# A decoder of two layers: the recurrence's second product is made in layer 0's feed-forward part, and the last part's first norm and whole numbers in cross attention 1

## The chip, the cores and the metric

The kernel runs on one core of one Trainium2 chip. The metric is the device time of one execution in microseconds (us). The core has five engines with a queue each, which work in the order of their programs and wait for one another by semaphores: TensorE (PE; its weight loads are PEld), VectorE (DVE), ScalarE (ACT), GpSimd (POOL) and SyncE (SP, which here only starts DMAs).

## What is computed

Input x is 4 x 1024 x 256 in f32, and a context of 4 x 77 x 192. Each of the two layers adds an attention part, a cross attention and a feed-forward part to x, with a norm after each:

```python
x = _layernorm(x + _L0_attn_ref(x, ...))     # causal attention, keys and values rounded
x = _layernorm(x + _L0_xattn_ref(x, ctx))
x = _layernorm(x + _L0_ffn_ref(x, ...))      # rounded weights and inputs, depthwise convolution, silu
x = _layernorm(x + _L1_attn_ref(x, ...))     # the recurrence below
x = _layernorm(x + _L1_xattn_ref(x, ctx))
x = _layernorm(x + _L1_ffn_ref(x, ...))

def _L1_attn_ref(x, A, B_w, B_b, C_w, C_b, D_w, D_b):
    Bu = x @ B_w.T + B_b
    Du = x @ D_w.T + D_b
    state = tanh(state * exp(A) + Bu[:, t])      # for t in 0..1023
    return states @ C_w.T + C_b + Du

def _L1_ffn_ref(x, ...):
    h = layernorm(x, ln1_g, ln1_b)               # with gain and bias
    h = bitlinear(h, w1, b1)                     # h rounded to 127 levels by its row maximum, w1 to -1, 0, 1
    h = gelu(h)
    h = layernorm(h, ln2_g, ln2_b)
    return bitlinear(h, w2, b2)
```

## The kernel before

The 4096 tokens are 32 tiles of 128 (NT = 32), kept in the SBUF tensor `X` (128 x 32 x 256, f32). The stages follow one another with barriers: projections, self attention, cross attention 0, layer 0's feed-forward part (`ffn0_and_recurrence`), the keys and cross attention 1 (`cross_layer1`), and the last part (`ffn1`). Each of the last three is a loop over slots j, written once for every engine; in slot j an engine works on several tiles at different depths (`a = j`, `b = j - 1`, and so on), and the order of the lines in each engine's function is the order of its queue. Nothing is reordered.

In `ffn0_and_recurrence` tile d = j - 4 ends the chain: the second product (L1462), the norm into `X[:, d]`, two transposes of it (L94), a copy `xT` by VectorE (L1531), the product with `BwT` (L1479) into bank 3, and VectorE writes it with a bias into `R.BU` (L1547), which feeds the recurrence. Behind L1479 in TensorE's queue stand, in the next slot, eight bf16 transposes of `f_hq` and eight f32 transposes of `f_g`, whose row maximum VectorE takes first (L140, `qF_amax`).

The recurrence is 1024 steps of two ScalarE operations on 128x1 (L763), the second half of the batch interleaved with the first. `R.act_states(n)` issues the next n steps; calls are strewn over the stages, 18 steps a slot in layer 0's part, 90 beside the keys and 15 a slot in cross attention 1.

In `cross_layer1` tile c = j - 1 is the recurrence's output: its `X` tile is turned (L94), copied by ScalarE (`iT`, L1717), multiplied by `DwT` (L1643, into bank 7), the states by `CwT` are added (L1645), VectorE adds `ib` (the tile plus constants, made by GpSimd, L1748) at L1687 and norms it into `X` (L128). Tile f = j - 3 is turned for the scores, sc = j - 4 has its scores (L1636), their maximum (L1690), subtraction (L1694) and exponential (L1727), p = j - 5 the sum (L1681), the division on GpSimd (L1742), eleven transposes (L1673) and a copy (L1735), and o = j - 6 the product of 11 f32 pieces into bank 7 (L1661), the addition of `xb` (L1703) and the norm. Both c and o use bank 7, so L1661 waits for L1687. Beside this the weights of the last part are rounded: `Ternary.pool` puts one step of half a weight matrix on GpSimd in six slots for each of the two (L702, L705, L710), `Ternary.pe` and `Ternary.act` turn and copy them.

`ffn1` waits for six vectors (`vec_in`). Tile a = j has the first norm with gain and bias (VectorE L111, L116, L118 and L128, GpSimd L123, L1930, L1933), b = j - 1 the maximum, scale and rounding to whole numbers (`q1`, L140 to L155), the turn, the first product (L1820) and the dequantising L1882, followed by Gelu; c = j - 2 the second norm (L1871, L1878), d = j - 4 the second rounding (`q2`), transposes and product L1828, and e = j - 5 the sum `j_y` (L1847) and the last norm. Each norm's reciprocal root is a power on GpSimd (L123, 128x1).

## Time and profile before

| | us |
|---|---|
| median of 3 runs | 2395.96 (2391.68 to 2397.53) |
| profiled execution, time | 2395.88 |
| its span, first to last instruction | 2394.2 |
| mean granted TensorE clock | 0.838 of full |

| busy in the span | us | share |
|---|---|---|
| TensorE matmuls | 1779.7 | 74% |
| VectorE | 1818.2 | 76% |
| ScalarE | 1348.5 | 56% |
| GpSimd | 884.4 | 37% |

```profile
## 2 busy tenths in 40 slices
PE   8849999999867777865556556568999998345544
DVE  4678888888348888867999999345666654799998
ACT  2105666666723443431588888999998942233333
POOL 2510000000038668543343333005535532455553
PEclk9958999999959988976777777569999999567666
```

Each digit is the busy share in one fortieth of the span (59.9 us) in tenths, and PEclk the TensorE clock that was granted. Layer 0's feed-forward part is about the slices 19 to 26 (1080 to 1530 us), the keys and cross attention 1 are 27 to 34 (to 2030 us), the last part 35 to 40. No engine is full over the whole; in each stage another one is, and so the profile has to be read stage by stage and within a stage by slots.

### The profile page before, as it was taken

How to read it: one execution, taken by the hardware profiler on the slowest of the kernel's cores; microseconds unless marked ns; L12 is line 12 of the kernel's file. 1: busy time of each engine (PE TensorE's matmuls, PEld its weight loads, DVE VectorE, ACT ScalarE, POOL GpSimd, SP SyncE). 2: the span in 40 equal slices, each digit the busy share in tenths (PEclk: the TensorE clock that was granted, in tenths of full speed). 3: DMA queues.
4: the chain of work that ended last, by engine and by line, in shares of the span. 5: the costliest groups of instructions: out<-in, count | busy, mean ns of one | idle time of the engine just before them, and what ended most of it. 6: DMA issues, size and time to landing. Idle time of an engine off the chain costs nothing. (4 is left out here: it accounts for less than half of the span.)

```text
span 2394.2 us, 36511 instructions
## 1 busy us (share of the span) xinstructions
PE 1779.7 (74%) x12168; PEld 1122.0 (47%) x12168; DVE 1818.2 (76%) x4605; ACT 1348.5 (56%) x3379; POOL 884.4 (37%) x951
## 2 busy tenths in 40 slices
PE   8849999999867777865556556568999998345544
PEld 4513333333346666654444444245667676133333
DVE  4678888888348888867999999345666654799998
ACT  2105666666723443431588888999998942233333
POOL 2510000000038668543343333005535532455553
PEclk9958999999959988976777777569999999567666
DMA  2011111111010000000000000100000000000000
GB/s 77 18 25 29 30 29 29 29 29 29 13 59 12 30 12 12 10 1 18 11 8 1 1 1 1 34 18 1 18 1 1 1 1 8 28 14 14 12 14 18
DMA packets 42808, 41.55 MB, mean 17 GB/s; under 512 B 16054, under 2 KB 34670, under 8 KB 42622
## 3 DMA queue, kind: packets, MB, share of 16 engines
q1 hardware_dynamic: 42622, 39.23, 6.1%
q8 instruction: 97, 1.59, 0.3%
q14 instruction: 89, 0.73, 0.1%
HBM read 22.03 MB, written 4.19 MB: 11 GB/s over the span
## 5 line engine op out<-in xcount | busy, mean ns | idle before, releaser
L763 ACT ACTIVATE ST<-ST,aexp 128x1 f32<-128x1 f32 x2046 | 583.1, 376 | 3.7 <-PEq L57 3.7
L597 ACT ACTIVATE PT<-PS 128x512 f32<-128x512 f32 x576 | 309.8, 597 | 219.5 <-PE PS L482 188.6
L558 DVE CUSTOM_DVE_ANT_0 junk<-PS,maskw 128x128 bf16<-128x128 f32 (+3 forms) x512 | 226.4, 486 | 33.8 <-PE PS L459 33.8
L459 PE MATMUL PS<-KT,QT 48*128 48x512 bf16 (+3 forms) x768 | 190.4, 351 | 54.1 <-DMA QT<-QS 33.0
L94 PE MATMUL PS<-ident,j_t 128*128 128x128 f32 x320 | 76.6, 423 | 170.8 <-ACT j_t L1900 142.2
L94 PE MATMUL PS<-ident,X 128*128 128x128 f32 x320 | 77.0, 328 | 154.4 <-DVE X L128 139.0
L561 DVE TENSOR_REDUCE MX<-PS 128x1 f32<-128x512 f32 x256 | 164.5, 684 | 27.7 <-PE PS L459 24.9
L501 PE MATMUL PS<-PT,VP 128*32 128x256 f32 (+1 forms) x2560 | 184.2, 370 | 0.0
L1661 PE MATMUL PS<-L_xattn_VW,l_pT 112*128 112x256 f32 x704 | 159.4, 382 | 9.3 <-DVE i_xb L1687 6.5
L631 POOL TENSOR_SCALAR nm<-MX 128x16 f32<-128x16 f32 x32 | 6.5, 203 | 431.1 <-DVE MX L564 431.1
L123 POOL TENSOR_TENSOR n_rs<-n_ve,neghalf 128x1 f32<-128x1 f32 x96 | 104.7, 1107 | 151.7 <-DVE n_ve L118 151.7
L459 PEld LDWEIGHTS PS<-KT,QT 48*128 48x128 bf16 x768 | 58.4, 94 | 200.2 <-issue 80.4
L94 PEld LDWEIGHTS PS<-ident,j_t 128*128 128x128 f32 x320 | 62.9, 222 | 183.4 <-ACT j_t L1900 152.5
L1661 PEld LDWEIGHTS PS<-L_xattn_VW,l_pT 112*128 112x128 f32 x704 | 131.2, 190 | 32.0 <-issue 12.1
L1636 PE MATMUL PS<-Q,l_xT 128*128 128x512 f32 (+1 forms) x384 | 141.0, 517 | 2.4 <-DVE l_s L1694 2.4
L476 PE MATMUL PS<-QT,KT 51*128 51x512 bf16 (+3 forms) x768 | 136.7, 331 | 0.0
L94 PEld LDWEIGHTS PS<-ident,X 128*128 128x128 f32 x320 | 40.2, 159 | 187.8 <-DVE X L128 152.7
L1209 PE MATMUL PS<-ident,d_s 128*112 128x128 f32 x352 | 66.1, 335 | 82.5 <-POOL d_s L1398 57.2
L1573 POOL TENSOR_TENSOR f_c<-f_h,f_cw 128x1024 f32<-128x1024 f32 x32 | 61.0, 1907 | 158.7 <-DVE f_h L1542 158.7
L1366 ACT COPY d_pT<-PS 112x768 f32<-112x768 f32 x32 | 25.5, 798 | 136.8 <-PE PS L1209 136.7
L1636 PEld LDWEIGHTS PS<-Q,l_xT 128*128 128x128 f32 x384 | 70.8, 194 | 66.0 <-issue 66.0
L1398 POOL TENSOR_TENSOR d_s<-d_s,d_den 128x1232 f32<-128x1232 f32 x32 | 71.9, 2247 | 79.2 <-DVE d_den L1313 79.2
(311 smaller groups left out, 4476.2 us busy)
## 6 DMA issues: line engine op xcount, KB each, us to landing
KT<-KS SPq DMA_DIRECT2D x192, 32.0 KB, 2.0
QT<-QS SPq DMA_DIRECT2D x192, 32.0 KB, 2.0
xs<-in_x SPq DMA_DIRECT2D x8, 512.0 KB
cx<-in_x SPq DMA_DIRECT2D x32, 128.0 KB, 2.0
out<-j_xn SPq DMA_DIRECT2D x32, 128.0 KB, 1.7
QT<-NMT SPq DMA_DIRECT2D x192, 2.0 KB
f_raw<-in_L_ffn_w SPq DMA_DIRECT2D x2, 1024.0 KB, 5.4
j_raw<-in_L_ffn_w SPq DMA_DIRECT2D x2, 1024.0 KB, 5.2
```

The costliest lines, as they stand in the source:

```text
L94: last = T.transpose(dst[:, i * P:(i + 1) * P], src[:, i * P:(i + 1) * P], idm[:, :])
L123: G.tensor_tensor(self.rs[u][:, :], self.ve[u][:, :], neghalf[:, :], ALU.pow).then_inc(self.rstd_done, 1)
L459: T.matmul(bank(u % 3)[:, 0:w * P], QT[i % R][rows, qt * P:(qt + 1) * P], KT[i % R][rows, k0 * P:(k0 + w) * P], start=True, stop=True).the ...
L476: last = T.matmul(bank(3 + (u0 + e) % 3)[:, at:at + w * P], KT[i % R][rows, kt * P:(kt + 1) * P], QT[i % R][rows, q0 * P:(q0 + w) * P], st ...
L501: last = T.matmul(bank(6 + first // 4)[32 * h:32 * h + 32, first % 4 * P:(first % 4 + hi - lo) * P], VP[:, v0:v0 + 32], PT[n % 4][:, h, lo ...
L558: V.tensor_tensor_reduce(junk[u % 3][:, 0:w * P], bank(u % 3)[:, 0:w * P], maskw[:, BANK - w * P:], 1.0, NEG, ALU.add, ALU.max, MX[i % 2][ ...
L561: V.tensor_reduce(MX[i % 2][:, e, slot:slot + 1], bank(u % 3)[:, 0:w * P], AX.X, ALU.max).then_inc(m_done, 1)
L597: C.activation(PT[n % 4][:, 2 * pr + e, 0:w], bank(3 + u % 3)[:, 0:w], ACT.Exp, scale=0.25).then_inc(e_done, 1)
L763: C.activation(self.ST[:, m, t:t + 1], self.ST[:, m, t - 1:t] if t else self.zero[:, :], ACT.Tanh, bias=self.BU[:, m, t:t + 1], scale=self ...
L1398: G.tensor_tensor(by_head(s[p % 4][:, :]), by_head(s[p % 4][:, :]), over_keys(den[p % 4]), ALU.mult).then_inc(d_p, 1)
L1636: last = T.matmul(PS[:, c0:end], xT[sc % 2][:, k * P:(k + 1) * P], x.M[:, k, sc % B, c0:end], start=k == 0, stop=k == KD - 1)
L1661: last = T.matmul(bank(7)[:, 0:D], pT[o % 2][:, i * P:(i + 1) * P], x.VW[:, i, o % B, :], start=i == 0, stop=i == VN - 1)
```

## The change

The product of X with D is made in layer 0's part. There TensorE multiplies the same `xT` by `DwT` behind the product with `BwT`, and VectorE adds the result to `X[:, d]`, with a new semaphore `f_du` that the next tile's second product also waits for, since both use bank 3. In cross attention 1 the transposes, the ScalarE copy and the D product of tile c fall away; what is left of it, the product of the states with `CwT`, goes to the front of TensorE's slot and into the free half of bank 3. The rings `ib`, `iT` and `xb` fall away too: the additions are made in `X` in place.

In the room that this frees cross attention 1 makes, for tile r = j - 7, the last part's first norm in one VectorE operation (gain times a reciprocal root that GpSimd works out from the variance already known, three operations on 128x1) and the bias on GpSimd, and for q = j - 8 the row maximum, scale and rounding, kept as bf16 in `JQ` with the levels in `LV`. The stage has one slot more. The last part starts from `JQ`: its first norm and first rounding are gone, its tiles are one to two slots closer together (NT + 3 slots instead of NT + 6), and the order of its VectorE operations within the slot changes. It waits for four vectors; the other two are loaded in cross attention 1.

The diff, cut to its core:

```diff
@@ ffn0_and_recurrence: pe, dve
                     if d >= 1:
                         T.wait_ge(R.fed, d)
+                        T.wait_ge(f_du, d)
...
                     for k in range(KD):
-                        last = T.matmul(bank(3)[rows(d), D:D + P], R.BwT[:, k, :], xT[d % 2][:, k * P:(k + 1) * P],
-                                        start=k == 0, stop=k == KD - 1)
+                        T.matmul(bank(3)[rows(d), D:D + P], R.BwT[:, k, :], xT[d % 2][:, k * P:(k + 1) * P],
+                                 start=k == 0, stop=k == KD - 1)
+                    for k in range(KD):
+                        last = T.matmul(bank(3)[:, 0:D], xT[d % 2][:, k * P:(k + 1) * P], R.DwT[:, k, :], start=k == 0, stop=k == KD - 1)
                     last.then_inc(f_bmm, 1)
...
+                    V.tensor_add(X[:, d, :], bank(3)[:, 0:D], X[:, d, :]).then_inc(f_du, 1)
@@ cross_layer1: sp, pe
+            for d, n in ((g1, "ln1_g"), (b1, "ln1_b")):
+                SP.dma_start(d[:, :], row("L1_ffn_" + n)).then_inc(vec_in, 16)
...
+                w1.pe_free(j - 1)
+                w2.pe_free(j - 1)
                 if on(c):
-                    transposes(X[:, c, :], bank(7), KD).then_inc(i_tr, 1)
+                    rows = slice(64 * (c % 2), 64 * (c % 2) + 64)
+                    T.wait_ge(R.step, 2 * P * (c // B + 1))
+                    if c >= 1:
+                        T.wait_ge(i_y, c)
+                    T.matmul(bank(3)[:, D:2 * D], R.ST[rows, (c % B) // 2, (c // B) * P:(c // B) * P + P], R.CwT[rows, :],
+                             start=True, stop=True).then_inc(i_mm, 1)
...
-                if on(c):
-                    T.wait_ge(i_xT, c + 1)
-                    for k in range(KD):
-                        T.matmul(bank(7)[:, 0:D], iT[c % 2][:, k * P:(k + 1) * P], R.DwT[:, k, :], start=k == 0, stop=False)
...
+                if c >= 0:
+                    T.wait_ge(i_y, min(c + 1, NT))
...
-                    if on(c):
-                        T.wait_ge(i_y, c + 1)
-                    else:
+                    if o >= 1:
                         T.wait_ge(d_y, o)
@@ cross_layer1: dve (new order: c's addition first, then p, sc, c's norm, o, q and r between)
                 if on(c):
                     V.wait_ge(i_y, c + 1)
-                    nI.dve_stats(c, ib[c % 2])
+                    nI.dve_stats(c, X[:, c, :])
                     nI.dve_moments(c)
-                    nI.dve_apply(c, X[:, c, :], ib[c % 2][:, :]).then_inc(i_xn, 1)
+                if on(q):
+                    V.wait_ge(l_b, q + 1)
+                    qJ.dve_max(q, l1[q % 2][:, :])
+                if on(c):
+                    nI.dve_apply(c, X[:, c, :], X[:, c, :]).then_inc(i_xn, 1)
+                if on(q):
+                    qJ.dve_level(q)
                 if on(o):
                     V.wait_ge(d_mm, o + 1)
                     V.wait_ge(d_xb, o + 1)
-                    V.tensor_add(xb[o % 4][:, :], bank(7)[:, 0:D], xb[o % 4][:, :]).then_inc(d_y, 1)
+                    V.tensor_add(X[:, o, :], bank(7)[:, 0:D], X[:, o, :]).then_inc(d_y, 1)
+                if on(q):
+                    qJ.dve_inverse(q)
...
+                if on(q):
+                    qJ.dve_scale(q, tmp[:, :], l1[q % 2][:, :])
+                if on(r):
+                    V.wait_ge(d_xn, r + 1)
+                    V.wait_ge(l_rs, r + 1)
+                    V.scalar_tensor_tensor(l1[r % 2][:, :], X[:, r, :], rs[r % 2][:, :], g1[:, :], ALU.mult, ALU.mult).then_inc(l_g, 1)
+                if on(q):
+                    qJ.dve_round(q, JQ[:, q, :], tmp[:, :]).then_inc(l_q, 1)
+                if on(o):
+                    nD.dve_apply(o, X[:, o, :], X[:, o, :]).then_inc(d_xn, 1)
@@ cross_layer1: act, pool
-                R.act_states(3)
-                if on(c):
-                    C.wait_ge(i_tr, c + 1)
-                    C.copy(iT[c % 2][:, :], bank(7)[:, 0:D]).then_inc(i_xT, 1)
-                R.act_states(6)
+                R.act_states(9)
...
                 if on(o):
                     nD.pool_rstd(o)
+                    if o >= 2:
+                        G.wait_ge(l_g, o - 1)
+                    G.wait_ge(nD.rstd_done, o + 1)
+                    G.tensor_scalar(ve[o % 2][:, :], nD.mv[o % 4][:, 1:2], nD.rs[o % 4][:, :], nD.rs[o % 4][:, :], ALU.mult, ALU.mult).then_inc(l_var, 1)
+                    G.wait_ge(l_var, 2 * o + 1)
+                    G.tensor_scalar(ve[o % 2][:, :], ve[o % 2][:, :], 1.0, EPS, ALU.mult, ALU.add).then_inc(l_var, 1)
+                    G.wait_ge(l_var, 2 * o + 2)
+                    G.tensor_tensor(rs[o % 2][:, :], ve[o % 2][:, :], neghalf[:, :], ALU.pow).then_inc(l_rs, 1)
+                if on(f):
+                    G.wait_ge(d_tr, f + 1)
+                    G.tensor_tensor(X[:, f, :], X[:, f, :], bo[:, :], ALU.add).then_inc(d_xb, 1)
+                if on(r):
+                    G.wait_ge(l_g, r + 1)
+                    G.tensor_tensor(l1[r % 2][:, :], l1[r % 2][:, :], b1[:, :], ALU.add).then_inc(l_b, 1)
                 w1.pool(j)
                 w2.pool(j)
@@ ffn1: the tiles of a slot; the order of VectorE's operations
-                b, d = j - 1, j - 4
+                b, d = j, j - 2
...
-                    transposes(t1[b % 2], bank(0), KD).then_inc(j_tr, 1)
+                    transposes(JQ[:, b, :], bank(0).bitcast(BF16), KD).then_inc(j_tr, 1)
...
-            for j in range(NT + 6):
-                a, b, c, d, e = j, j - 1, j - 2, j - 4, j - 5
+            for j in range(NT + 3):
+                b, c, d, e = j, j - 1, j - 2, j - 3
...   # d's maximum and levels, e's j_y as before
+                if on(c):
+                    V.wait_ge(j_gelu, c + 1)
+                    n2.dve_stats(c, h[c % 3])
                 if on(e):
                     V.wait_ge(n_y, e + 1)
                     n3.dve_stats(e, y[e % 2])
...   # moments of c, moments of e, then c's L1871
+                if on(e):
+                    n3.dve_apply(e, xn[e % 4][:, :], y[e % 2][:, :]).then_inc(n_xn, 1)
                 if on(c):
                     V.wait_ge(n2.rstd_done, c + 1)
...   # c's L1878, b's L1882
-                    q1.dve_scale(b, t1[b % 2][:, :], l1[b % 4][:, :])
...
-                    n1.dve_apply(a, l1[a % 4][:, :], X[:, a, :]).then_inc(j_ln, 1)
```

## Rows read from the trace of the kernel before

**Rows 1.** Table of windows, one in each of three stages; us, busy us (instructions) by engine, granted clock, DMA.
```profile
1200.00:1300.00 100.00, 61.32 (x414) 49.23 (x412) 93.50 (x246) 87.36 (x291) 38.79 (x33) 0.75 0.00 1
1800.00:1927.00 127.00, 124.59 (x558) 89.74 (x557) 83.51 (x143) 114.02 (x339) 67.81 (x56) 1.00 0.00 1
2200.00:2360.00 160.00, 81.11 (x339) 51.69 (x337) 153.63 (x380) 57.40 (x61) 86.15 (x94) 0.69 0.04 13
```

**Rows 2.** Timeline, one slot of layer 0's part: start, us, engine, line, idle before.
```profile
1371.97 1.11 PE L1479 MATMUL PS<-f_xT,BwT 128*64 128x128 f32 x4 [0.83 <-DVE f_xT L1531]
...
1373.84 1.91 PE L94 MATMUL PS<-ident,f_g 128*128 128x128 f32 x8
...
1375.80 1.22 DVE L140 TENSOR_REDUCE qF_amax<-PS 128x1 f32<-128x1024 f32 x1 [0.64 <-PE PS L94]
...
1385.18 1.11 PE L1479 MATMUL PS<-f_xT,BwT 128*64 128x128 f32 x4 [0.83 <-DVE f_xT L1531]
```

**Rows 3.** Table of windows, two microseconds of that slot, for the granted clock.
```profile
1374.00:1375.00 1.00, 1.00 (x7) 1.00 (x6) 0.94 (x3) 1.00 (x5) 1.00 (x1) 0.50 0.00 0
1376.00:1377.00 1.00, 1.00 (x16) 0.94 (x14) 1.00 (x2) 1.00 (x5) 1.00 (x1) 1.00 0.00 0
```

**Rows 4.** Line L1643: ns least/median/most of one record.
```profile
L1643 PE MATMUL PS<-DwT,i_xT x128: 379/379/797, 1592.2 to 1974.7; 128*128 128x256 f32 x128
```

**Rows 5.** Timeline, its first block of four records in cross attention 1.
```profile
1592.16 2.08 PE L1643 MATMUL PS<-DwT,i_xT 128*128 128x256 f32 x4 [9.98 <-ACT i_xT L1717]
```

**Rows 6.** Timeline, TensorE in one slot of cross attention 1.
```profile
1778.78 0.38 PE L94 MATMUL PS<-ident,X 128*128 128x128 f32 x2
...
1783.14 1.03 PE L1643 MATMUL PS<-DwT,i_xT 128*128 128x256 f32 x4
...
1784.72 0.44 PE L94 MATMUL PS<-ident,X 128*128 128x128 f32 x2
...
1785.40 0.89 PE L1661 MATMUL PS<-L_xattn_VW,l_pT 112*128 112x256 f32 x3 [0.24 <-DVE i_xb L1687]
```

**Rows 7.** Table of windows, one whole slot of cross attention 1.
```profile
1841.17:1853.82 12.65, 12.41 (x57) 8.95 (x56) 8.70 (x15) 11.44 (x36) 8.45 (x7) 1.00 0.00 1
```

**Rows 8.** Timeline, ScalarE's copy of tile c in that slot.
```profile
1845.29 0.35 ACT L1717 COPY i_xT<-PS 128x256 f32<-128x256 f32 x1
```

**Rows 9.** Timeline, GpSimd in that slot.
```profile
1843.09 3.70 POOL L702 TENSOR_SCALAR j_raw<-j_raw,j_w2T_inv 128x1024 f32<-128x1024 f32 x1
...
1852.82 0.73 POOL L1748 TENSOR_TENSOR i_xb<-X,cd 128x256 f32<-128x256 f32 x1
```

**Rows 10.** Timeline, starts of two slots and the drained end of the last part.
```profile
2208.27 1.28 DVE L1871 SCALAR_TENSOR_TENSOR Q<-Q,n_mv,j_g 128x1024 f32<-128x1024 f32 x1
...
2218.63 1.28 DVE L1871 SCALAR_TENSOR_TENSOR Q<-Q,n_mv,j_g 128x1024 f32<-128x1024 f32 x1
...
2368.05 1.28 DVE L1882 SCALAR_TENSOR_TENSOR Q<-PS,j_ds,j_bh 128x1024 f32<-128x1024 f32 x1
...
2369.56 1.21 DVE L140 TENSOR_REDUCE q_amax<-Q 128x1 f32<-128x1024 f32 x1
...
2374.08 1.28 DVE L1871 SCALAR_TENSOR_TENSOR Q<-Q,n_mv,j_g 128x1024 f32<-128x1024 f32 x1
2374.24 2.05 POOL L123 TENSOR_TENSOR n_rs<-n_ve,neghalf 128x1 f32<-128x1 f32 x2 [6.91 <-DVE n_ve L118]
...
2375.81 1.28 DVE L1878 SCALAR_TENSOR_TENSOR Q<-Q,n_rs,j_b 128x1024 f32<-128x1024 f32 x1 [0.44 <-POOL n_rs L123]
...
2377.33 1.21 DVE L140 TENSOR_REDUCE q_amax<-Q 128x1 f32<-128x1024 f32 x1
```

**Rows 11.** By lines, the norm of c: busy us, mean ns; idle before it, releaser.
```profile
L128 DVE TENSOR_SCALAR X<-i_xb,nI_mv,nI_rs 128x256 f32<-128x256 f32 x32 | 25.8, 806 | 21.4 <-POOL nI_rs L123 21.4
```

**Rows 12.** Timeline, VectorE's first operation of the last part, with its wait.
```profile
2040.01 0.43 DVE L111 BATCH_NORM_STATS2 n_six<-X 128x6 f32<-128x256 f32 x1 [8.41 <-DMA j_bo<-in_L_ffn_b]
```

**Rows 13.** Line L1847: ns least/median/most, start of the first and of the last.
```profile
L1847 DVE SCALAR_TENSOR_TENSOR j_y<-PS,j_ds,j_xb x32: 472/474/485, 2079.5 to 2388.9; 128x256 f32<-128x256 f32 x32
```

More of the change, by code:

```diff
@@ L1801, in pe @@
         def pe():
-            for j in range(NT + 5):
-                b, d = j - 1, j - 4
+            for j in range(NT + 2):
+                b, d = j, j - 2
                 if on(d):
@@ L1904, in act @@
                         C.wait_ge(j_mm, b - 1)
-                    C.activation(xqT[b % 2][:, :], bank(0)[:, 0:D], ACT.Identity, bias=down[:, :], scale=1.0).then_inc(j_xqT, 1)
+                    C.copy(xqT[b % 2][:, :], bank(0).bitcast(BF16)[:, 0:D]).then_inc(j_xqT, 1)
                 if on(d):
@@ L1923, in pool @@
                 if on(a):
-                    n1.pool_rstd(a)
                     if a >= 6:
```

150 lines of the change are left out of this document (56 added, 94 removed).

## Prediction

> **What bounds the kernel now.** I read the table of windows first [rows 1], because the three stages that the change touches have three different limits. In the feed-forward part of layer 0 VectorE is busy 93.5 us of 100 and TensorE 61.3 at a granted clock of 0.75. In cross attention 1 TensorE is busy 124.6 us of 127 at full clock, ScalarE (the recurrence's tanh) 114.0, VectorE only 83.5 and GpSimd 67.8. In the last part VectorE is busy 153.6 us of 160. So moving VectorE work out of the last part into cross attention 1, and TensorE work out of cross attention 1 into layer 0's part, is sound if the cover is real; each of the three has to be priced from its own slot (one turn of the loop over j).
>
> **Layer 0's feed-forward part: the product X times D is added (loss).** The timeline of one slot [rows 2] shows VectorE waiting 0.64 us for the eight f32 transposes of f_g; they end at 1375.75 and the maximum starts at 1375.80. These transposes stand in TensorE's queue behind L1479, which can't start before the normed X is turned and copied. So from L1479 (1371.97) to the end of the transposes (3.8 us) TensorE is on the path, although it idles elsewhere in the slot, and the new matmuls are put exactly between. The window over it has the granted clock at 0.50, which is the lower level, 1.2 GHz; the one two us later has 1.00 [rows 3]. The same product in cross attention 1 has matmul records of 379 ns at best and 797 ns at worst [rows 4], and the block of four took 2.08 us at the lower level behind an idle TensorE [rows 5] and 1.03 us at the higher one [rows 6]. Behind L1479 there is no start-up, so I take 1.75 us at the lower level. Since TensorE works longer in one stretch, the clock will in some slots be up before the transposes of f_g are through; those took 1.91 us at the lower level [rows 2], so at most half of that comes back. Estimate: 0.4 us back on average, so +1.35 us a slot, with bounds of 1.0 (higher clock) and 1.75 (none back). The added VectorE addition on 256 columns is some 0.4 us, as the statistics of 256 columns [rows 12]; it lies in the wait that the longer TensorE stretch makes, and costs nothing; it also lets the next second product wait on f_du, which is long set by then. If the product cost nothing, that addition would cost its 0.4 us. 32 slots: **+43 us**, bounds +30 and +56.
>
> **Cross attention 1: what leaves.** TensorE's slot is 12.65 us with 12.41 busy [rows 7]. It loses the transposes of tile c (0.38 us, of which some 0.25 are not overlapped), the D product (1.03, some 0.95) and the wait for VectorE's i_xb in front of the big product: L94 starts at 1784.72 with 0.44 us of work, L1661 at 1785.40 [rows 6], 0.4 us more than it need. 12.65 - 0.25 - 0.95 - 0.4 = 11.05 us. The recurrence's engine is then next: ScalarE has 11.44 us in that slot and loses only the 0.35 us copy [rows 7, 8]. That gives 11.1 to 11.2; eight slots have a weight copy on top, so I take 11.4 us, a gain of 1.25 us.
>
> **Cross attention 1: what comes.** VectorE gets seven operations on 128x256 or smaller (maximum, scale, round, multiplication by the gain, and two on one column), five of some 0.4 us and two of some 0.15, 2.3 us. 8.70 busy [rows 7] becomes 11.0 without overlaps, and some 10.3 with them, since back-to-back operations overlap by about 0.1 us each. It is covered, barely. GpSimd gets two operations on one column, a third power of minus one half (two of the last part took 2.05 us together, the second alone about 0.5 [rows 10]) and an addition of 0.73 us [rows 9]: 1.7 us. In an ordinary slot it has 4.8 us of work (8.45 less the 3.70 of L702 [rows 7, 9]) and becomes 6.5. But in twelve slots it also carries a step of the weights' rounding, up to 3.70 us [rows 9]: 10.2 us, and in these it stops twice for VectorE (variance of c, variance of o) with VectorE waiting for it right behind. I price these two stops at 1 us each and take 12.4 us for those slots, a gain of 0.2. Of the 26 slots in which all stages run 11 are such. 15 x 1.25 + 11 x 0.2 = 21. At the start of the loop ScalarE's states set the pace and c's copy leaves, some 3.5 us; at its end one more slot is added, in which the last tile's gain, bias, maximum, scale and rounding run one after the other, also some 3.5 us. Together **-21 us**, bounds -40 (11.1 everywhere) and 0 (VectorE and GpSimd give all of it back). The two loads on SP's queue stand behind the first weights and ahead of a load that waits anyway; their first use is seven slots later. The wait on the recurrence's step moves to the front of TensorE's slot; the states are a chunk ahead there.
>
> **The last part: what leaves.** A slot takes 10.36 us (2208.27 to 2218.63 [rows 10]). The trace shows the new slot almost as it will be, because in the drained slots the first norm and its rounding are absent: from maximum to maximum 7.77 us (2369.56 to 2377.33), without the product's L1882, which adds 1.28 less its overlap, 1.20 [rows 10]. 8.97 us. Two corrections. In the new order the statistics of c don't wait behind those of e, 0.35 us less. And the order puts the norm of e right behind L1871: its power stands in GpSimd's queue behind c's, so it comes to run during L1871. In these rows a power that started 0.16 us into L1871 was through 0.4 us after it had ended (the pair took 2.05 us and L1878 waited 0.44). This stall is already in the 7.77; but once it ends GpSimd goes on at once with the addition of bo, and beside such an addition VectorE's norm of 256 columns takes 0.81 us [rows 11], twice the 0.4 that I have for 256 columns: +0.4. **9.05 us a slot**, bounds 8.5 (no contention) and 9.6.
>
> **The last part: the sum.** VectorE is released at 2040.0 after a wait of 8.41 us for the six vectors [rows 12]. The last L1882 starts at 2368.05 [rows 10], 328.0 us later. New: the whole numbers are there, so h(0) comes at 0.3 us, h(1) some 6.6 later, h(2) 8.8 later, then 29 slots of 9.05: 15.7 + 262.5 = 278.2, so 49.8 less. From L1882 to the last j_y there are 20.9 us now (to 2388.9 [rows 13]); the loop has one drained slot less, 3.7 off. Two vectors of 128 KB less of 1.9 MB in 8 us is 1.0 off. **-54.5 us**, bounds -38 (9.6) and -70 (8.5).
>
> **Against a rule of the skill.** L1878 starts at 2375.81, released by c's power; the pair of powers ends at 2376.29, so e's power started just before L1878, ran beside it in some 0.5 us, and L1878 took its usual 1.28 [rows 10]. Neither held the other up. The Trainium skill, "SBUF — State Buffer", section "SBUF: two separate sides", says that GpSimd and certain VectorE operations share one pair of ports as an exclusive lock, held for the whole instruction by whichever started first. By that rule the start of L1878 beside e's power should not have been possible, so the row speaks against it here; what it would make of the new order is the third rival.
>
> **The rivals.**
> 1. The product in layer 0's part is cheap, because the clock comes up early or doesn't fall between slots: 30 us instead of 43, 2350. For it: longer TensorE stretches. Against: the mean granted clock of this part is 0.75 although TensorE has a long stretch in every slot [rows 1], and the stretch priced here comes first after its idle time, at 0.50 [rows 3].
> 2. No contention in the last part, 8.5 us a slot: 29 x 0.55 = 16 less, 2347. Against it: the rows with 2.05 and 0.81.
> 3. The powers hold L1871 up too: c's power starts 0.16 us behind L1871 now [rows 10]; in the new order two operations of e, some 0.3 us, stand between the variance and L1871, so it will start some 0.15 us ahead of it. If L1871 has to wait for its rest, 0.5 less 0.15, and e's power with it, a slot is 9.5 us and the time 29 x 0.45 = 13 more, 2376. Against it: L1878 at 2375.81, as above.
> 4. Cross attention 1 gains nothing, 2384, because ScalarE, now next in line, waits for VectorE's subtraction, which is late by the seven operations.
> 5. Slower. In cross attention 1 GpSimd and VectorE hand over to each other four times a slot (two powers, the new variance, the bias), with VectorE's scale, gain and rounding in a row just when o's power wants to run. From 13.1 us a slot on the gain of the last part is eaten up (26 x 0.45 + 43 = 54.7 against 54.5); at 13.9 us, which is 1.5 us more than I have for the slots in which GpSimd rounds weights, 26 x 1.25 = 33 are lost and the time is 2417. Against it: the sum of VectorE's work is 10.3.
> 6. The change doesn't do what it says: the first product stays late in the slot. TensorE's program order excludes that.
>
> **The numbers.** 2395.9 + 43 - 21 - 54.5 = 2363.4. The profiled execution has a span of 2394.2 and a time of 2395.88, the median of the runs is 2395.96, so the sum needs no shift. Chances: forecast (2352 to 2374) 0.42, rival 1 0.14, rival 2 0.12, rival 3 0.10, rival 4 0.13, rival 5 0.07, a mixture about zero 0.02. A measurement of this kernel can tell about 0.3% from no change, 7.2 us. Of rival 4 and of losses that add up, 0.08 fall within that. Faster 0.85, same 0.08, slower 0.07. The range takes in rivals 1 to 4 and the bounds of the product: 2334 to 2392.
>
> **What would show it.** The interval between two starts of L1479's successor 14.6 us instead of 13.2 and a longer wait of qF_amax for TensorE; in cross attention 1 11.4 us between two results of the big product, with ScalarE busy nearly throughout, and 12.4 where GpSimd rounds weights; in the last part 9.05 us a slot, the idle time of VectorE in front of the norm of e with GpSimd's power as its releaser, and a first j_y some 19 us after the vectors have landed instead of 39.5. Wrong would be above all a slot of cross attention 1 over 12.6, or one of layer 0's part under 14.

## The result and the profile after

The changed kernel takes 2318.6 us (median of four runs, 2315.4 to 2322.4) beside 2396.7 for the kernel before (2391.7 to 2398.2): ratio 0.9678, 95% interval 0.9654 to 0.9702, 78 us less. The forecast was 33 us less, and its range ended at 2334. The profiled execution has a span of 2313.6 us, 80.6 under that of before. By the stages' first loads on SyncE's queue, which mark their starts:

| stretch | before | after | difference | forecast |
|---|---|---|---|---|
| to the start of cross attention 1 | 1581.7 | 1593.0 | +11.3 | +43 |
| cross attention 1 | 449.7 | 415.3 | -34.4 | -21 |
| last part | 362.8 | 305.3 | -57.5 | -54.5 |

Windows of the changed kernel, columns as in [rows 1]:

```profile
1200.00:1300.00 100.00, 63.87 (x403) 48.58 (x404) 88.80 (x247) 83.91 (x276) 36.25 (x33) 0.74 0.02 6
1800.00:1900.00 100.00, 97.56 (x429) 69.11 (x428) 79.16 (x181) 95.64 (x284) 77.13 (x86) 1.00 0.00 1
2100.00:2200.00 100.00, 57.27 (x250) 35.33 (x248) 92.73 (x180) 40.83 (x46) 28.84 (x35) 0.70 0.05 15
```

The limits are the same three engines. In layer 0's part VectorE's share fell by five points: it waits more, but not as much more as forecast. In the last part GpSimd fell from 54 to 29 in 100.

Timeline of the changed kernel, the slot that answers [rows 2]:

```profile
1380.73 1.12 PE L1480 MATMUL PS<-f_xT,BwT 128*64 128x128 f32 x4 [0.83 <-DVE f_xT L1534]
1381.77 2.07 PE L1483 MATMUL PS<-DwT,f_xT 128*128 128x256 f32 x4
...
1384.41 1.04 PE L94 MATMUL PS<-ident,f_g 128*128 128x128 f32 x8
...
1383.88 0.36 DVE L1550 TENSOR_SCALAR ST<-PS,bb 64x128 f32<-64x128 f32 x1 [1.34 <-PE PS L1483]
1384.27 0.42 DVE L1552 TENSOR_TENSOR X<-PS,X 128x256 f32<-128x256 f32 x1
...
1385.49 1.22 DVE L140 TENSOR_REDUCE qF_amax<-PS 128x1 f32<-128x1024 f32 x1
```

The product (L1483) takes 2.07 us, dearer than the 1.75 of the sum. But the transposes of f_g behind it take 1.04 us where they took 1.91, and the maximum follows with no wait. The granted clock over product and transposes, as in [rows 3]:

```profile
1382.00:1383.00 1.00, 1.00 (x3) 0.82 (x4) 0.55 (x2) 1.00 (x5) 0.37 (x1) 0.50 0.00 0
1384.60:1385.40 0.80, 0.80 (x8) 0.62 (x6) 0.80 (x3) 0.80 (x4) 0.79 (x1) 1.00 0.00 0
```

The product runs at the lower level (0.50), the transposes at the higher (1.00). VectorE's wait has moved: it no longer stands in front of the maximum but in front of L1550 (1.34 us), which waits until the product too is done.

One ordinary slot of cross attention 1 (answers [rows 7]) and, below it, one of the four long ones, from one start of the big product (L1663) to the next, in which GpSimd rounds weights:

```profile
1770.50:1781.63 11.13, 11.13 (x51) 8.05 (x50) 9.00 (x21) 11.13 (x35) 6.69 (x9) 1.00 0.01 2
1843.71:1855.75 12.04, 11.31 (x51) 7.96 (x50) 8.98 (x21) 11.06 (x34) 10.20 (x11) 1.00 0.00 1
```

TensorE has no idle time in the ordinary slot, nor has ScalarE; in the long one TensorE idles 0.73 us. The last part (answers [rows 10]):

```profile
2153.96 1.28 DVE L1884 SCALAR_TENSOR_TENSOR Q<-Q,n_mv,j_g 128x1024 f32<-128x1024 f32 x1
2155.75 0.73 DVE L128 TENSOR_SCALAR j_xn<-j_y,n_mv,n_rs 128x256 f32<-128x256 f32 x1 [0.51 <-POOL n_rs L123]
2156.41 1.27 DVE L1892 SCALAR_TENSOR_TENSOR Q<-Q,n_rs,j_b 128x1024 f32<-128x1024 f32 x1
```

and GpSimd beside it:

```profile
2153.85 1.80 POOL L123 TENSOR_TENSOR n_rs<-n_ve,neghalf 128x1 f32<-128x1 f32 x2 [6.45 <-DVE n_ve L118]
2155.62 0.72 POOL L1932 TENSOR_TENSOR j_xb<-X,j_bo 128x256 f32<-128x256 f32 x1
```

The pair of powers, the idle 0.51 us in front of e's norm and the long norm (0.73) are as forecast. First and last result, to set beside [rows 13]:

```profile
L1870 DVE SCALAR_TENSOR_TENSOR j_y<-PS,j_ds,j_xb x32: 473/475/484, 2035.3 to 2308.5; 128x256 f32<-128x256 f32 x32
```

The slot is 8.94 us.

### The profile page after: what moved, and what is told of

It is laid out like the page before. It is cut to its first block and busy times, and to the rows that moved or that the text cites. A ratio compares the mean times of both kernels' runs of the same rounds, so it can differ in the third digit from the quotient of the medians.

```text
span 2313.6 us, 36269 instructions
## 1 busy us (share of the span) xinstructions
PE 1758.1 (76%) x12104; PEld 1097.3 (47%) x12104; DVE 1782.5 (77%) x4542; ACT 1333.4 (58%) x3347; POOL 847.5 (37%) x983
## 5 line engine op out<-in xcount | busy, mean ns | idle before, releaser
L94 PE MATMUL PS<-ident,X 128*128 128x128 f32 x256 | 64.0, 339 | 143.7 <-DVE X L128 129.6
L1663 PE MATMUL PS<-L_xattn_VW,l_pT 112*128 112x256 f32 x704 | 157.4, 379 | 2.9 <-issue 2.9
L1663 PEld LDWEIGHTS PS<-L_xattn_VW,l_pT 112*128 112x128 f32 x704 | 131.2, 190 | 20.0 <-issue 3.4
L94 PE MATMUL PS<-ident,j_t 128*128 128x128 f32 x256 | 56.7, 394 | 109.8 <-ACT j_t L1906 109.8
L123 POOL TENSOR_TENSOR n_rs<-n_ve,neghalf 128x1 f32<-128x1 f32 x64 | 58.0, 922 | 214.8 <-DVE n_ve L118 214.8
L94 PEld LDWEIGHTS PS<-ident,X 128*128 128x128 f32 x256 | 35.1, 166 | 166.5 <-DVE X L128 143.1
L1563 ACT ACTIVATE f_g<-f_g 128x1024 f32<-128x1024 f32 x32 | 33.9, 1058 | 121.0 <-DVE f_g L1494 121.0
L94 PEld LDWEIGHTS PS<-ident,j_t 128*128 128x128 f32 x256 | 44.6, 203 | 121.0 <-ACT j_t L1906 121.0
```

What stands on the lines that cost most here:

```text
L94: last = T.transpose(dst[:, i * P:(i + 1) * P], src[:, i * P:(i + 1) * P], idm[:, :])
L123: G.tensor_tensor(self.rs[u][:, :], self.ve[u][:, :], neghalf[:, :], ALU.pow).then_inc(self.rstd_done, 1)
L1663: last = T.matmul(bank(7)[:, 0:D], pT[o % 2][:, i * P:(i + 1) * P], x.VW[:, i, o % B, :], start=i == 0, stop=i == VN - 1)
```

## Experiments: what the product costs in layer 0's part

**The change's first half alone.** The kernel before with the product moved and nothing of the norm:

```diff
 ffn0:   + D product behind the BwT product, tensor_add into X, f_du
 cross1: - transposes(X[:, c, :]), ScalarE's copy iT, the D product
         the product of the states with CwT stays behind the scores, in bank 7
```

> The kernel before with the first half of the change alone: D's product and the addition in layer 0's part, no transposes, no copy and no D in cross attention 1; the last part's first norm and whole numbers stay in the last part. If the two halves add up: +11.3 us up to the start of cross attention 1 as in the changed kernel, there 5 us from the start of the stage, 35.7 us from the slots and 4 us more because the norm's work is not in them, no longer tail, and nothing in the last part: 33 us shorter than before, 2362 to 2366. By the recorded sum (+43 in layer 0's part, 24.5 off in cross attention 1) the same kernel would take 2412 to 2418. If the slots of cross attention 1 gain only because the stage's VectorE order was written anew with the norm's work: 2380 to 2395.

Measured: 2373.2 us beside 2399.0, ratio 0.9894 (0.9868 to 0.9921), span 2370.5. The three stretches differ from before by +9.0, -34.0 and +1.3 us. So 23.7 us of the gain is the product's, and the norm's half brings the other 56.9 of the span (2370.5 to 2313.6) at no net cost to cross attention 1. The recorded sum had +43 - 24.5 for this half and would have been 42 us too high; for the norm's half it had 51 with its tail, 6 too few. **So most of the miss of 48 us lies in the product's half.** How much depends on a term that belongs to both: if the 12.4 us for the slots with rounding is charged to the norm's work, which was its reason, the halves missed by 31 and 17 us. My additive expectation of 2362 to 2366 was 9 us too low: this kernel's slots of cross attention 1 are 11.56 us and not 11.1, where TensorE keeps the old order, with a wait in it:

```profile
1763.87 0.70 PE L1644 MATMUL PS<-CwT,ST 64*128 64x256 f32 x2
1764.50 0.44 PE L94 MATMUL PS<-ident,X 128*128 128x128 f32 x2
1765.18 4.99 PE L1660 MATMUL PS<-L_xattn_VW,l_pT 112*128 112x256 f32 x22 [0.24 <-DVE i_xb L1686]
```

In the changed kernel the product of the states stands in front of the scores, and this wait is gone. A run further down that has the new order and none of the norm's work has ordinary slots of 11.13, so the 0.43 us come with the order (and the bank); which of its pieces brings them isn't shown beyond the wait of 0.24.

**No product, half of one, one, two; no addition.** The edits to the changed kernel:

```diff
 p0:  - the four matmuls with DwT (the addition stays)
 half:  matmul(bank(3)[:, 0:P], xT, DwT[:, k, 0:P])
 p1:  - tensor_add(X, bank 3, X), - T.wait_ge(f_du, d)
 p2:    for k in (0, 1, 0, 1): matmul(bank(3)[:, 0:D], ...)
```

> The changed kernel without the product of X with D in layer 0's part; the addition stays and adds whatever stands in the bank, so the last state is left out of the output's meaning. The changed kernel's slot is 13.66 us against 13.24 of the kernel before. Theory A (the 0.42 us are VectorE's addition, and the product is hidden): the slot stays at 13.6 to 13.7 and the time within 4 us of the changed kernel's 2318.6. Theory B (the 0.42 us are what is left of the product, the addition lies in VectorE's wait for the transposes of f_g): the slot falls to 13.2 to 13.3, the part ends 13 to 17 us earlier, and the time is 5 to 12 us shorter, since the recurrence's states on ScalarE set the end.

> The changed kernel with the product of X with D over half of D's columns alone (the other half of the addition adds what stood in the bank; the output is not the reference's). So far the slot of layer 0's part is 13.3 us with no product, 13.66 with one and 15.15 with two. If the cost grows in proportion up to one product (0.37 us for 1.98 us of TensorE): 13.45 to 13.5, and a time of 2309 to 2311. If the slot keeps with the pattern of the granted clock (13.66 with one product at two equal stretches of either level): half a product falls either to the 13.3 of none or to 13.6. If each microsecond before the transposes of f_g counted in full beyond a slack of 1.6 us: 13.3, the time of no product, 2301 to 2304.

> The changed kernel with the product of X with D but without VectorE's addition of its result and without TensorE's wait for it (the term D x is left out of the output). Theory A (the addition sets the slot): the slot falls from 13.66 to 13.2 to 13.3 us. Theory B (the product sets it): the slot stays at 13.6 to 13.7. If both matter: between.

> The changed kernel with the product of X with D issued twice over in each slot of layer 0's part (its result is then twice as large; 2.07 us more work at the lower clock, 1.03 at the higher). Theory A (a product in this place is hidden because the granted clock comes up before the transposes of f_g): the first product used the slack up, so the second costs 0.8 to 1.1 us a slot, at the higher clock: slot 14.5 to 14.8, time +25 to +35 us. Theory B (a product costs 0.42 us a slot, in proportion): slot 14.0 to 14.1, time +10 to +15 us. The recorded prediction's price, 1.35 to 1.75 us for each, would give 15.0 to 15.4 and +45 to +55 us.

(The second product doesn't double the result, as that expectation says: its sum starts anew and overwrites the first.) Measured (the four edited kernels in two runs each, with 2396.9 and 2399.1 us for the kernel before beside them). The second column is the mean interval over all 32 f_y. The slot and the columns behind it are means over the 21 slots from the eighth f_y to the twenty-ninth, in which the recurrence runs and nothing is drained:

| kernel | time | f_y, mean interval | slot | VectorE waits for TensorE | sixteen taps | D product | f_g transposes |
|---|---|---|---|---|---|---|---|
| before | 2396.7 | 12.99 | 13.31 | 0.74 | 5.33 | - | 1.84 |
| addition alone | 2301.4 | 12.99 | 13.30 | 0.53 | 5.29 | - | 1.88 |
| half | 2313.8 | 13.37 | 13.66 | 1.44 | 4.62 | 1.22 | 1.85 |
| one (changed) | 2318.6 | 13.50 | 13.66 | 1.44 | 4.63 | 2.07 | 1.06 |
| one, no addition | 2316.8 | 13.46 | 13.66 | 1.72 | 4.63 | 2.08 | 1.05 |
| two | 2360.7 | 14.82 | 15.15 | 3.02 | 4.63 | 3.56 | 1.19 |

Theory A fell: the addition costs nothing, as forecast. The price is the product's, and it is no line: 0.4 us a slot for half of it, nothing for the other half, 1.5 for a second one, which is more than the forecast had for the first. The second half is free because of the clock: 0.85 us more of product, 0.79 less of transposes. A second product finds them at the higher clock already and wins nothing. That left the first half: it adds 0.91 us of waits and the slot grows by only 0.36. The column that moves the other way is VectorE's sixteen steps of the convolution's outer taps, 0.67 us shorter.

**The taps and GpSimd.** Kernel before, VectorE's taps and maximum, and GpSimd's two steps of the middle tap:

```profile
1387.09 1.91 POOL L1573 TENSOR_TENSOR f_c<-f_h,f_cw 128x1024 f32<-128x1024 f32 x1 [5.00 <-DVE f_h L1542]
1389.07 1.90 POOL L1575 TENSOR_TENSOR f_c<-f_c,f_cb 128x1024 f32<-128x1024 f32 x1
...
1389.01 1.22 DVE L140 TENSOR_REDUCE qF_amax<-PS 128x1 f32<-128x1024 f32 x1 [1.01 <-PE PS L94]
1390.15 2.81 DVE L1491 SCALAR_TENSOR_TENSOR f_g<-f_h,f_cw,f_c 128x128 f32<-128x128 f32 x8
```

Changed kernel:

```profile
1382.63 1.90 POOL L1577 TENSOR_TENSOR f_c<-f_h,f_cw 128x1024 f32<-128x1024 f32 x1 [4.74 <-DVE f_h L1545]
1384.61 1.90 POOL L1579 TENSOR_TENSOR f_c<-f_c,f_cb 128x1024 f32<-128x1024 f32 x1
...
1386.63 2.18 DVE L1494 SCALAR_TENSOR_TENSOR f_g<-f_h,f_cw,f_c 128x128 f32<-128x128 f32 x8
```

GpSimd's steps start when f_h is made. Before, they run until 1390.97, and the first tap starts at 1390.15; of the eight, it alone is long, 969 ns against 340, so it lasts until just after GpSimd has ended. In the changed kernel the wait for the product stands between f_h and the taps, GpSimd is through at 1386.51, the taps start at 1386.63, and eight take 2.18 us instead of 2.81. By lines (ns least/median/most), the first taps of before, and then of the changed kernel:

```profile
L1491 DVE SCALAR_TENSOR_TENSOR f_g<-f_h,f_cw,f_c x184: 333/339/1417, 1203.4 to 1498.1; 128x128 f32<-128x128 f32 x184
```

```profile
L1494 DVE SCALAR_TENSOR_TENSOR f_g<-f_h,f_cw,f_c x176: 341/344/348, 1208.8 to 1497.6; 128x128 f32<-128x128 f32 x176
```

Before, the long tap is there in 22 of the 23 slots of this stretch, and in each of the 22 it ends 0.15 us behind GpSimd's step. In the changed kernel not one of 176 is long any more; GpSimd is through only 0.05 to 0.34 us before the first tap, a margin that nobody had planned. To test it, GpSimd's two steps were cut to 8 of 128 positions, with the product and without:

```diff
- G.tensor_tensor(c0[:, :, :],   h[:, :, 1:P + 1], cw, mult)   # and the same for the bias
+ G.tensor_tensor(c0[:, :, 0:8], h[:, :, 1:9],     cw, mult)
```

> Layer 0's part without the product of X with D, and with GpSimd's two steps of the convolution over 8 of 128 positions (product and most of the middle tap are left out; not the reference's output). Its twin without the second cut has a slot of 13.26 us, in which VectorE's sixteen steps of the outer taps take 5.38 us and the first eight run beside GpSimd's second step. Theory P (GpSimd in flight makes VectorE's taps slower, and the product's price is low because it moves the taps behind GpSimd's steps): the taps fall to 4.6 and the slot to 12.5 to 12.9. Rival (the taps' length follows something else, so the low price is the clock's alone): taps 5.3 to 5.4, slot 13.2 to 13.3.

> The changed kernel, product in its place, with the same cut of GpSimd's convolution steps (most of the middle tap is left out). The changed kernel has taps of 4.61 us already and a slot of 13.66. Theory P: with nothing left to win on the taps the slot stays at 13.5 to 13.7, so that without GpSimd in the way one product costs 0.8 to 1.1 us a slot, against 0.40 with it. Rival (the clock alone): the difference between this slot and its twin's without the product stays 0.4.

Measured: 2279.6 us without the product (slot 12.59, f_y every 12.35 us), 2310.3 with it (slot 13.66, 13.53), the slots again over the 21 full ones. With GpSimd out of the way **one product costs 1.07 us a slot**, as theory P said (0.8 to 1.1); with GpSimd's steps in place it costs 0.36. The difference is 0.71 us, and the taps account for it: without the product the sixteen take 4.63 us now instead of 5.29, and that slot falls from 13.30 to 12.59. The rival, the clock alone, is out: these two keep the clock's pattern (transposes of f_g 1.86 and 1.06 us) and not the low price. Over the whole kernel one product costs 30.6 us here and 17.2 with GpSimd's steps. That is more than 21 slots explain, since the first seven intervals of f_y, in which the recurrence is only starting, grow by 1.6 and 0.75 us each; no run shows why. The long first tap is gone:

```profile
L1494 DVE SCALAR_TENSOR_TENSOR f_g<-f_h,f_cw,f_c x176: 341/345/348, 1207.9 to 1474.3; 128x128 f32<-128x128 f32 x176
```

**The product taken off the path.** Same work, the product a slot later, behind the transposes of f_g; its addition behind the maximum:

```diff
 TensorE: hq transposes(d), f_g transposes(c),
+         wait R.fed > e; D product(e = d - 1)
          second product(d), first product(a), ..., BwT product(d)
 VectorE: maximum(c)
+         wait f_dmm > e; tensor_add(X[:, e, :], bank 3)
          taps
```

> The changed kernel with the same work, but the product of X with D issued one slot later, behind the transposes of f_g, and its addition behind the maximum over them. Theory P and the path (a product costs only what it puts before the transposes of f_g, and VectorE's wait for them): the slot falls to 13.2 to 13.4 as with no product, the time to 2298 to 2306. Rival (the addition now waits for the product, up to 2 us at the lower clock, and the second product of the feed-forward part comes late for f_y): slot 13.7 to 14.6, time 2318 to 2345.

Measured: 2311.4 us, f_y every 13.28 us; the slots run between 13.0 and 13.8, 13.49 over the 21 full ones. Somewhat under half of what the product costs is won back (7.2 of 17.2 us), less than expected. VectorE waits 0.33 us for the late product and 0.71 for the transposes, and the held tap is back in 7 of 22 slots, each time ending 0.14 to 0.15 us behind GpSimd's step:

```profile
L1496 DVE SCALAR_TENSOR_TENSOR f_g<-f_h,f_cw,f_c x176: 335/344/1744, 1206.9 to 1492.1; 128x128 f32<-128x128 f32 x176
```

## Experiments: cross attention 1 and the last part

**Without the norm's work in cross attention 1.**

```diff
- VectorE: gain, maximum, scale, round; GpSimd: variance, power, bias; one slot
+ VectorE once: memset(JQ), memset(LV)
```

> The changed kernel without the last part's first norm and whole numbers in the slots of cross attention 1 (they are left out; the last part works on ones). Theory 1 (TensorE alone sets the slot of 11.35 us, the added work of VectorE and GpSimd is free): the slots stay at 11.3 to 11.4, only the tail behind the last slot is 4 to 6 us shorter: time 5 us shorter. Theory 2 (the added work delays the slots, by GpSimd's powers and VectorE's rounding): slots of 10.9 to 11.1 and the slots with the weights' rounding at 11.4 instead of 12.1: time 15 to 20 us shorter.

Measured: 2307.6 us. By the starts of TensorE's big product (L1663), the four slots of 12.04 to 12.20 fall to 11.13 and the ordinary ones stay at 11.13; those with a weight's transposes have 11.36 to 11.44, and one 11.84. From the first big product to the last there are 338.1 us instead of 342.1, and from there to the end of the stage 9.2 instead of 15.3. (The fill of JQ takes VectorE 6.9 us at the start; the 25 us wait described below absorbs it.) So the added work costs some 4 us in the slots and 6 in the tail, 10.3 of the stage and 11.0 of the time. That lies between the theories: in the ordinary slots the work is free (theory 1), in the long ones it isn't (theory 2).

**GpSimd's rounding steps at 64 of 1024 columns.**

```diff
- G.tensor_scalar(half(raw, k), half(raw, k), inv, 1.0, mult, min)     # and the two like it
+ G.tensor_scalar(half(raw, k)[:, 0:64], half(raw, k)[:, 0:64], inv, 1.0, mult, min)
```

> The changed kernel with GpSimd's twelve steps of rounding the last part's weights over 64 of 1024 columns (most of the weights is left out, the output is not the reference's). In cross attention 1 eight slots take 12.05 to 12.2 us where the others take 11.3. Theory G (GpSimd's long steps hold up what GpSimd owes the slot: the power of the norm, the division): these eight slots fall to 11.3 to 11.4, the stage ends 5 to 7 us sooner. Theory T (TensorE's and ScalarE's own work for the weights, or the DMA, makes them long): they stay at 12.0 to 12.2.

Measured: 2312.9 us. The long slots fall to 11.13 (theory G; where the weights' transposes begin, one slot takes 12.02). The expectation counts eight; by TensorE's big product there are four, the other steps of rounding leave the slot at 11.1 to 11.4. In the long slots of the changed kernel the division stands behind a step of 3.6 to 3.7 us, and TensorE's transposes of its result wait for it, 0.73 to 0.89 us:

```profile
1843.40 3.64 POOL L705 TENSOR_SCALAR j_raw<-j_raw 128x1024 f32<-128x1024 f32 x1
1847.01 2.25 POOL L1760 TENSOR_TENSOR l_s<-l_s,l_den 128x1232 f32<-128x1232 f32 x1
1849.35 1.38 PE L1675 MATMUL PS<-ident,l_s 128*112 128x128 f32 x11 [0.73 <-issue]
```

With the norm's work left out the same steps of rounding cause no such wait, so it takes both. The stage gains 3.9 us (411.4 for 415.3). The time of the profiled execution hardly shows it, because the stage starts 3.3 us later there; 2.2 of these are already there at the first f_y, ahead of anything that the edit touches.

**ScalarE's states dealt out otherwise.** At the start of cross attention 1 in the changed kernel ScalarE works off 54 steps before it copies the first turned tile:

```profile
1593.06 30.14 ACT L763 ACTIVATE ST<-ST,aexp 128x1 f32<-128x1 f32 x108 [1.02 <-PEq L57]
1623.12 0.34 ACT L1741 COPY l_xT<-PS 128x256 f32<-128x256 f32 x1
```

```diff
 ffn0:   act_states(9) twice a slot  ->  act_states(10) twice
 cross1: 9 + 3 + 3 a slot            ->  0 in slots 0 to 3, then 9 + 3 + 3
```

> The changed kernel with the same work, but the recurrence's states dealt out otherwise on ScalarE: 20 instead of 18 in a slot of layer 0's part, none in slots 0 to 3 of cross attention 1 (where 54 of them, 30 us, stand ahead of the first copy of transposed tokens, which TensorE waits 25 us for). Theory S (the states set that start and ScalarE has room in layer 0's slot of 13.66): cross attention 1 has its fifth recurrence product 18 to 22 us sooner, layer 0's slot stays at 13.7, and the time is 2296 to 2302. Rival: ScalarE becomes the bound of layer 0's slot (20 states 11.4 us, silu 1.06, the weights' copy 0.6 to 0.8: about 13.1, with its waits over 13.66): slot 13.9 or more, 7 to 10 us of the gain lost, time 2303 to 2312.

Measured: 2299.0 us. The interval between VectorE's third and fourth addition of a recurrence product falls from 24.99 to 3.70 us; layer 0's slot stays at 13.66. ScalarE had the room.

**The order in the last part.** Two edits, together and one by one:

```diff
 late apply: VectorE ..., L1884, L1892, L1896 (h), then the norm of e
 w1 first:   TensorE transposes JQ(b), product w1(b), then transposes t2(d), product w2(d)
             ScalarE copy xqT(b) before t2(d)
```

> The changed kernel with two changes of order in the last part: VectorE applies the last norm behind h instead of before the second step of the second norm, and TensorE and ScalarE make the transposes and the w1 product of tile b before the transposes of t2. Theory V (VectorE's chain sets the slot of 8.94: it waits 0.51 for the power of the last norm and 0.3 for the w1 product): slot 8.0 to 8.3, time 2292 to 2298. Rival (the ring from h through Gelu on ScalarE, the second norm, t2, its transposes and y sets it, and the new order lengthens that by making t2 wait behind the copy): slot 8.6 to 9.0, time 2310 to 2319. Slower, if TensorE's w1 product at the lower clock (1.9 us) comes in front of the transposes of t2 each time: slot over 9.0.

> The changed kernel with only VectorE's last norm applied behind h in the last part. Its wait for the power (0.51 us) goes; the slot of 8.94 falls to 8.4 to 8.5 if nothing stands behind it; to 8.6 to 8.8 if TensorE's w1 product, which then ended 0.3 us before h, comes late next.

> The changed kernel with only TensorE's and ScalarE's order changed in the last part (w1's product of tile b before the transposes of t2). If VectorE's wait for the power is the only one in the slot, it stays at 8.9 to 9.0; the gain of 0.73 us a slot with both would then be mostly the other edit's. If the order alone carries it: 8.2 to 8.5.

Measured: both 2296.0 us, slot 8.21. Order alone (one run): 2315.4, slot 8.94, nothing. Late apply alone (one run): 2317.0, slots between 8.20 and 9.03, 8.7 on average; in a slot of 9.02 VectorE waits 0.72 us for the w1 product in front of h. Its last part is 7.7 us shorter all the same (297.6 for 305.3); the time doesn't show it, because the stages ahead, which the edit leaves as they are, took longer in that run (first f_y 5.6 us later). **They remove two waits that end nearly together: alone they pay nothing and 0.24 us a slot, both 0.73.** VectorE in the version with both:

```profile
2102.34 1.28 DVE L1884 SCALAR_TENSOR_TENSOR Q<-Q,n_mv,j_g 128x1024 f32<-128x1024 f32 x1
2103.72 1.28 DVE L1888 SCALAR_TENSOR_TENSOR Q<-Q,n_rs,j_b 128x1024 f32<-128x1024 f32 x1
2104.93 1.28 DVE L1892 SCALAR_TENSOR_TENSOR Q<-PS,j_ds,j_bh 128x1024 f32<-128x1024 f32 x1
2106.12 0.40 DVE L128 TENSOR_SCALAR j_xn<-j_y,n_mv,n_rs 128x256 f32<-128x256 f32 x1
```

No wait is left, and the norm of e takes 0.40 us, GpSimd being quiet beside it.

**Together**, without and with the late product:

> The changed kernel with both reorderings together: the states dealt out otherwise (19.5 us shorter alone) and the two changes of order in the last part (22.6 us alone). If they are independent: 2275 to 2279, a ratio to the kernel before of 0.949 to 0.951. If one takes the other's gain (the last part's slot rises again, or the stages between give it back): 2285 to 2296.

> The kernel with the states dealt out otherwise and the two changes of order in the last part (2280.1 us), and the product issued one slot later as in the run before this one. If the late product wins 12 to 17 us alone and ScalarE's 20 states a slot (11.4 us, with silu and a copy about 13.1) find room in a slot of 13.3: 2263 to 2269. If ScalarE then sets the slot: 13.5 or more and 2270 to 2280.

Measured: 2280.1 us, ratio to before 0.9503 (0.9482 to 0.9524), and **2272.5 us, 0.9482 (0.9466 to 0.9498)**, the fastest here, 46 us under the changed kernel. The first lacks 3.7 us of the sum of the single gains (19.6 and 22.6, of two runs each). In its start of cross attention 1 TensorE idled 4.12 us and then ran at the lower clock:

```profile
1627.20 2.60 PE L1675 MATMUL PS<-ident,l_s 128*112 128x128 f32 x11 [4.12 <-ACT l_xT L1741]
1629.72 1.22 PE L1639 MATMUL PS<-CwT,ST 64*128 64x256 f32 x2
1630.87 5.83 PE L1648 MATMUL PS<-Q,l_xT 128*128 128x512 f32 x12
```

where the version with the states alone idled 2.45 us and stayed at the higher one:

```profile
1626.25 1.41 PE L1675 MATMUL PS<-ident,l_s 128*112 128x128 f32 x11 [2.45 <-ACT l_xT L1741]
1627.59 0.70 PE L1639 MATMUL PS<-CwT,ST 64*128 64x256 f32 x2
1628.22 4.40 PE L1648 MATMUL PS<-Q,l_xT 128*128 128x512 f32 x12
```

The difference, 3.1 us, is most of the 3.7. The version with the late product has the same 4.12 us of idle time there and the same slow stretch (2.60, 1.22 and 5.70 us). It wins 7.6 us by the late product instead of 12 to 17; its slot is 13.49, with VectorE's waits as in the late product's own run.

## Why the prediction was wrong, step by step

The forecast was 48 us too high: 32 of them in layer 0's part, 13 in cross attention 1, 3 in the last part.

**Layer 0's part, +43 forecast, +11.3 measured: the step that failed.** Its slot is 13.66 us and not 14.6, one of the two signs of being wrong that the forecast named.
- *Price of the product, 1.75 us at the lower clock.* It took 2.07 in every slot; right in kind, too low.
- *"At most half comes back, 0.4 us on average."* Mis-sized. The transposes went from 1.84 to 1.06 us, 0.78 back. With the longer stretch the rise comes ahead of them in nearly every slot; I took the scatter of before for the scatter of after. The two errors nearly cancel: with some 0.2 us of overlap the maximum starts 1.06 us later behind the start of the product with `BwT` (4.81 us for 3.75, means of 21 slots), where the forecast had 1.35.
- *The path ends at the maximum.* Here the forecast missed a term, and this is most of the miss. It followed TensorE to the maximum and not VectorE beyond it, where the first tap was held until GpSimd's step had ended (969 ns for 340). The product's wait lets GpSimd finish: 0.70 us a slot. 1.06 - 0.70 is 0.36, and the slot grew by 0.35. Without GpSimd's steps the product costs 1.07 a slot, as much as the maximum is late there (4.82 for 3.74).
- *VectorE's addition costs nothing.* Right, by the run without it (13.66 either way) and the one without the product (13.30, for 13.31 before).
- *32 slots.* The part's last f_y is 15.0 us later, cross attention 1 starts 11.3 later. That the stage between absorbs the rest was not in the sum; by the mean interval, 0.51 us times 31 are 15.9.

**Cross attention 1, -21 forecast, -34.4 measured.**
- *Start, 3.5 us:* 5.0. *Tail, +3.5:* +6.2.
- *Slots.* From TensorE's first big product to its last 377.7 us became 342.1, 35.6 less or 1.37 us a slot over the 26 in which all stages run; the forecast had 21. The 1.25 that I took for ordinary slots was too little: 12.65 became 11.13, and with a weight's transposes 13.07 or 12.87 became 11.36. Mis-sized above all was the rest: I gave 0.2 us to 11 slots in which GpSimd rounds weights. Four were long, 12.04 to 12.20 instead of 12.4, and gained 0.5 us each; the other steps of rounding cost next to nothing. The wait was also another than the one priced: not VectorE's for a power, but TensorE's for the division, which GpSimd makes late.
- *ScalarE as the next bound.* Both are without a gap in the ordinary slot, but TensorE sets it: past the last state ScalarE is busy only 2.9 to 3.5 us of a slot, and the slots keep their 11.13 and 11.34.

**The last part, -54.5 forecast, -57.5 measured.** Right term by term, within some tenths. Slot 8.94 for 9.05; the vectors' wait 6.96 instead of 8.41 (1.45 less for 1.0); last h to last j_y 16.8 us for 17.2; h(0) at 0.9 us instead of 0.3. The stall in front of e's norm is 0.51 us and the norm 0.73 beside GpSimd's addition.

**The rivals.** Rival 1 (cheap product, 2350) is what happened, and further: its reason, the clock, is the smaller part of it, and I gave it 14 in 100 and only 13 us. Rival 2 fell: the contention in the last part is there, and taking it out brings 8.21 together with TensorE's order. Rival 3 fell: the pair of powers started 0.11 us ahead of L1884 (2153.85, 2153.96), and L1884 took its usual 1.28. Rival 4 fell: cross attention 1 gained 34 us. Rival 5 fell: past the start no slot of cross attention 1 is over 12.2 us by TensorE's big product. Rival 6 fell.

**VectorE and GpSimd in each other's way.** Measured: a first tap that starts 0.82 us before GpSimd's step ends takes 969 ns, 340 otherwise, and between 1203 and 1498 us such taps take up to 1417. A held tap ends 0.15 us behind GpSimd's end. That is what the Trainium skill, "SBUF — State Buffer", section "SBUF: two separate sides", says of VectorE operations with two SBUF inputs beside a GpSimd operation that reads SBUF: whichever starts first has the port pair for the whole instruction. By that rule the trace of this stage agrees. The forecast had set it aside on the strength of powers on one column and didn't ask it of the two 1.9 us steps in layer 0's part. For those powers the rows go one way against it and one way with it. A power that is already running doesn't hold VectorE (L1884 at 1.28 with a power begun 0.11 us ahead). But a power that starts while VectorE's 1.28 us step is running does wait: it takes 0.55 us otherwise, and here 1.54 in the kernel before (beside L1871, which starts at 2103.96) and 1.28 in the changed one (beside L1884, from 2153.96), each time ending 0.4 us after VectorE's step:

```profile
2104.12 1.54 POOL L123 TENSOR_TENSOR n_rs<-n_ve,neghalf 128x1 f32<-128x1 f32 x1 [3.83 <-DVE n_ve L118]
```

```profile
2154.36 1.28 POOL L123 TENSOR_TENSOR n_rs<-n_ve,neghalf 128x1 f32<-128x1 f32 x1
```

The second of these is the power that e's norm waits 0.51 us for. So the stall that the forecast took from its rows as a length (2.05 for the pair) is this hold; with 0.55 us the power would have been through before L1884 was. The maximum, which reads bank memory, took its usual 1.22 beside GpSimd.

## What to carry to other kernels

When work is put in front of a wait, follow the waiting engine on to its next operations: what it now starts later may come clear of a neighbour that held it up, and that part of the wait is free. Price the first dose and not a line: here half a product, one and two cost 0.4, 0.4 and 1.9 us a slot. Count slots only where the loop is full: a stretch that takes in the drained end makes the slot look shorter. If two waits in a slot end nearly together, try the edits that remove them together before judging either.

## What the runs showed of the hardware

- VectorE's step on two SBUF tensors, begun while GpSimd has a 1.9 us step in flight, lasts until 0.15 us after that step's end (340 ns becomes 969, at most 1417 in the stretch looked at and 1744 with the late product); a reduction over PSUM beside it doesn't (1.22 us).
- The other way round, a GpSimd power on one column, 0.55 us otherwise, took 1.54 and 1.28 us when it began 0.16 and 0.40 us into a VectorE step of 1.28 us on two SBUF tensors. Begun 0.11 us ahead of such a step, it took 0.55 and the step its 1.28.
- A whole product put ahead of the same transposes brought the granted clock from 0.50 to 1.00 before they ran, in nearly every slot (1.84 to 1.06 us), half a product didn't (1.85); the product itself stays at the lower level, 2.07 us against 1.03 at the higher [rows 6].
- After 4.12 us of idle time TensorE's next 9.3 us ran at a mean granted clock of 0.65 and the same matmuls took some 3 us longer than after 2.45 us of it; two events of the first and one of the second, so the two numbers bracket no rule.
